# Dealing ratio steps by a fixed table, a later place for the next batch's sigmoids, and an input quantisation without GpSimd

## The chip, the core and the metric

The kernel runs on one core of one Trainium2 chip. The metric is the device time of one execution in microseconds (us). The engines of the core are TensorE (PE in the rows; PEld is its weight load), VectorE (DVE), ScalarE (ACT), GpSimd (POOL) and SyncE (SP, which only issues DMAs). Each works through its own instructions in order, and they wait for one another on semaphores.

## The reference, cut to what matters

Four batches of 512 tokens with 512 channels pass through four sub-layers, each fed by a gate "cond" and each added to x:

```python
x = x + L0_attn(L0_cond(x, f, f, w, u, cond))      # gated linear attention
x = x + L0_ffn(L0_cond2(x, f, f, w, u, cond))      # 16 experts, top 6, plus a shared one
x = x + L1_attn(L1_cond(x, f, f, w, u, cond))      # state space layer, weights quantised to 4 bits
x = x + L1_ffn(L1_cond2(x, f, f, w, u, cond))      # MXFP8 feed-forward
```

Each cond is `sigmoid(x) * ratio`, where the ratio does not depend on x: it is a quotient of exponentials of f, summed by a decaying scan in both directions. The last feed-forward quantises its inputs in blocks of 32:

```python
def _mx_dequant(t):
    blocks = t.reshape(rows, feat // 32, 32)
    scales = maximum(max(abs(blocks), axis=-1) / 448.0, 1e-30)
    q = (blocks / scales[..., None]).astype(float8_e4m3fn).astype(float32)
    return (q * scales[..., None]).reshape(rows, feat)
h = silu(mx(x) @ mx(gate_w).T) * (mx(x) @ mx(up_w).T)
out = mx(h) @ mx(down_w).T
```

## The kernel before

Everything is written out by hand, one instruction stream for each engine. There are three stages.

**Stage 1** is the attention and the routing, batch by batch. The change leaves it alone.

**Stage 2**, from about 1285 to 2435 us, runs 63 expert tiles (`NTL`) of 256 tokens each. In tile j TensorE does these in order: gate and up projections (line 964, 48 matmul records), the input transposes of tile j+1 (L959), the weight transposes of side work (L984), and the down projection of tile j-1 (L975). Two kinds of side work ride along in tiles 0 to 59:

- **Ratio steps.** The second layer's ratios are computed as 16 units of six steps each, 96 in all; `ratio_steps(j)` says which steps belong to tile j. VectorE does `ratio_step(r)`. Steps 0 and 3 start with exponentials from ScalarE (`ratio_exps`, L1245 to L1249, which needs another activation table than the expert's Silu) and go on with four scans; steps 1 and 4 are three elementwise operations; steps 2 and 5 are a reciprocal (L1722), a product, and then the clipped input for the next exponentials (`r_min2` after step 2; `ratio_start` with `r_min` after step 5). So ScalarE's part of step 3 needs VectorE's step 2, and its part of the next unit's step 0 needs VectorE's step 5. Before, 96 steps are spread evenly over 60 tiles, so that a tile has one or two.
- **Preparation of weights.** 74 blocks are quantised and transposed; `prep_tiles(j)` gives one or two of them to a tile. In 14 of the 60 tiles there are two (j = 4, 8, 12, 17, 21, 25, 29, 34, 38, 42, 47, 51, 55, 59). The first 26 blocks have four groups to a row (lighter on VectorE), the rest have blocks of 32. VectorE scales and rounds them in tile j after the ratio steps, and TensorE transposes them in tile j+1. Where there are two, they pass through one PSUM bank: the second transpose waits until ScalarE has copied out the first (L1446).

ScalarE's order in a tile is what the prediction leans on: two Silus, the scaling of this tile's preparation blocks (`scale_groups`, L1402 to L1407, which waits for VectorE's scales), the copies of the next tile's input (L1415), then `ratio_exps`, and only then the copies of the transposed blocks (L1446), and last the expert's output.

**Stage 3**, from about 2435 us on, takes each batch through the state space layer and the feed-forward. The feed-forward has 16 blocks (i = 0 to 15, four groups of weights by four token tiles). For each, TensorE multiplies the gate (L1219) and up (L1225) halves and transposes the previous block's quantised product (L1199); the down projection (L1206) follows in a lump after blocks 5, 9, 13 and at the end. ScalarE does the Silu (L1538) and the copy out of the transposes (L1544). VectorE multiplies (L2301) and quantises (L1652 to L1673). TensorE may begin the gate half of block i+1 only after ScalarE's Silu of block i.

Into this loop the next batch's start is woven: GpSimd gathers the routed expert outputs (`collect`), VectorE sums them (`weigh`, blocks 5, 7, 9, 11) and adds them to x (`add_routed`, L2117, blocks 7, 9, 11, 13), ScalarE takes the sigmoid (`sigmoid2`, L1454, blocks 8, 10, 12, 14), and VectorE multiplies by the ratio (`gate2`).

The feed-forward's own input is quantised in four token tiles before and during the first blocks: TensorE transposes (L1173), VectorE does `quantise_x` up to the addition of the rounding constant (L2294), GpSimd subtracts it again (L1631) and multiplies by the scale (L1636), and TensorE transposes back (L1184).

Of the kernel before, what the change touches and what calls it, by code (L numbers as in the profile page):

```python
# [20 lines left out]
ALU = mybir.AluOpType  # L21
# [3 lines left out]
P = 128  # L25
NB, T, D = 4, 512, 512
NC = D // P
NT = T // P
# [22 lines left out]
QB = 32  # L51
# [76 lines left out]
def build(nc, A, out, scratch_fq, scratch_mx):  # L128
# [11 lines left out]
    with ctx:  # L140
# [226 lines left out]
        f_vx = ev("f_vx", NT)  # L367
        f_qx = ev("f_qx", NT)
# [15 lines left out]
        def r3(ap, n):  # L384
            return ap.rearrange("p (a n) -> p a n", n=n)
# [123 lines left out]

        LAST = NTL - 3  # L510

        def ratio_steps(j):

            a, b = (NB * NC * 6 * min(i, LAST) // LAST for i in (j, j + 1))
            return range(a, b)

        def prep_tiles(j):

# [734 lines left out]
        def _(act):  # L1253
# [198 lines left out]
            def sigmoid2(b, k):  # L1452
                act.wait_ge(x2_ready.sem, x2_ready.at(b, k + 1))
                act.activation(tile_of(hT, k), tile_of(X2[b % 2], k), ACT.Sigmoid).then_inc(sig2.sem, 1)  # L1454
# [4 lines left out]
            for b in range(NB):  # L1459
                act.wait_ge(s_proj.sem, s_proj.at(b, 1))  # L1460
                act.activation(vt, bank(2)[64:64 + SH, :], ACT.Copy).then_inc(s_raw.sem, 1)
                for i in range(2):
                    q = act.activation(bsq[:, i, :], bank(i, SN), ACT.Square)
                q.then_inc(s_sq.sem, 1)
                act.activation(th, bank(2, SN), ACT.Copy)
                act.activation(lamt, bank(2)[96:96 + SH, :], ACT.Sigmoid).then_inc(s_th.sem, 1)
                act.wait_ge(s_v.sem, s_v.at(b, 1))
                act.activation(nab, nab, ACT.Exp)
                act.drain()
                act.activation(nab, nab, ACT.Ln, bias=one[0:SH, :]).then_inc(s_ln.sem, 1)  # L1470
                for i in range(NT * 4):
                    if i == 2:
                        act.wait_ge(s_ms.sem, s_ms.at(b, 1))
                        for q in range(2):
                            mm = act.activation(brs[:, q, :], bank(3 + q, SN), ACT.Sqrt, bias=eps_rms[0:SN, :])
                        mm.then_inc(s_rms.sem, 1)
                        act.wait_ge(s_cs.sem, s_cs.at(b, 1))
                        act.activation(eat, eat, ACT.Exp).then_inc(s_ea.sem, 1)
                    if i == 6:
                        act.wait_ge(s_ang.sem, s_ang.at(b, 1))  # L1480
                        act.activation(trg[:, :, :], nrd[:, :, :], ACT.Sin).then_inc(s_sin.sem, 1)
                    if i == 13:
                        act.wait_ge(s_tmc.sem, s_tmc.at(b, 1))
                        act.activation(eL, csl, ACT.Exp)
                        act.activation(dend, dend, ACT.Exp)
                        act.activation(r3(ecs, SH), tm[:, :, 2, :], ACT.Exp).then_inc(s_exps.sem, 1)
                    k, h = i // 4, i % 2
                    act.wait_ge(s_xz.sem, s_xz.at(b, i + 1))
                    if i % 4 < 2:
                        q = act.activation(xh[k][:, h * 512:(h + 1) * 512], bank(6 + h), ACT.Silu)  # L1490
                    else:
                        q = act.activation(ynT8[:, 4 * h:4 * h + 4, k * P:(k + 1) * P], r3(bank(6 + h), P), ACT.Silu)
                    q.then_inc(s_silu.sem, 1)

                def decay_exp(k, g):
                    act.wait_ge(s_diff.sem, s_diff.at(b, k * 4 + g + 1))
                    act.activation(Md[:, g % 2, :], Md[:, g % 2, :], ACT.Exp).then_inc(s_exp.sem, 1)

                def normalise(k):
                    act.wait_ge(s_yr.sem, s_yr.at(b, k + 1))  # L1500
                    act.activation(Yt[k % 2], Yt[k % 2], ACT.Copy, scale=ss[:, 2:3]).then_inc(s_yn.sem, 1)

                def y_evacuate(k):
                    act.wait_ge(s_tr.sem, s_tr.at(b, k + 1))
                    for i in range(2):
                        q = act.activation(ynT8[:, 4 * i:4 * i + 4, k * P:(k + 1) * P], r3(bank(2 + i), P), ACT.Copy)
                    q.then_inc(s_ynT.sem, 1)

                for k in range(NT):
                    if k:  # L1510
                        normalise(k - 1)
                    decay_exp(k, 0)
                    if k:
                        y_evacuate(k - 1)
                    decay_exp(k, 1)
                    decay_exp(k, 2)
                    decay_exp(k, 3)
                    act.wait_ge(s_y.sem, s_y.at(b, k + 1))
                    act.activation(Dx, Yt[k % 2], ACT.Square, accum_out=ss[:, 0:1])
                    act.drain()  # L1520
                    act.activation(ss[:, 1:2], ss[:, 0:1], ACT.Sqrt, bias=eps_rms, scale=1.0 / DI).then_inc(s_yss.sem, 1)
                normalise(NT - 1)
                y_evacuate(NT - 1)
                for k in range(NT):
                    act.wait_ge(x3_ready.sem, x3_ready.at(b, k + 1))
                    act.activation(tile_of(hT, k), tile_of(X2[b % 2], k), ACT.Sigmoid).then_inc(sig3.sem, 1)

                for i in range(FB * NT + 1):
                    if b + 1 < NB and i >= 8 and i % 2 == 0 and i < 16:
                        sigmoid2(b + 1, (i - 8) // 2)  # L1530
                    if i < NT:
                        act.wait_ge(f_tq.sem, f_tq.at(b, i + 1))
                        act.activation(xqT[:, :, i * P:(i + 1) * P], r3(bank(6), P), ACT.Copy).then_inc(f_xT.sem, 1)
                    if i < FB * NT:
                        act.wait_ge(f_gate.sem, f_gate.at(b, i + 1))
                        if i >= 2:
                            act.wait_ge(f_mul.sem, f_mul.at(b, i - 1))
                        act.activation(fs[i % 2], bank(4), ACT.Silu).then_inc(f_silu.sem, 1)  # L1538
                    if i:
                        ib, t = (i - 1) // NT, (i - 1) % NT  # L1540
                        act.wait_ge(f_tr.sem, f_tr.at(b, i))
                        if t == 0 and ib >= 2:
                            act.wait_ge(f_down.sem, f_down.at(b, ib - 1))
                        act.activation(hqT[ib % 2][:, :, t * P:(t + 1) * P], r3(bank(6), P), ACT.Copy)\  # L1544
                           .then_inc(f_hT.sem, 1)


        @block.gpsimd
        def _(pool):
# [41 lines left out]
            def collect(b):  # L1591

                for n in range(NTK):
                    k = b * NTK + n
                    if k >= NYG:
                        pool.wait_ge(y_acc.sem, k - NYG + 1)
                    pool.indirect_dma_start(yg[k % NYG], None, d_y,
                                            bass.IndirectOffsetOnAxis(ap=physu[:, k:k + 1], axis=0))\
                        .then_inc(y_rows[k % NYG].sem, 16)
# [6 lines left out]
            for b in range(NB):  # L1606
# [18 lines left out]
                        per_head(state, state, eL[0:SN, hs]).then_inc(s_sdec.sem, 1)  # L1625


                for t in range(NT):
                    v, m = fxv[t % 2], fxm[t % 2]
                    pool.wait_ge(f_vx.sem, f_vx.at(b, t + 1))  # L1630
                    pool.tensor_tensor(v, v, m, ALU.subtract)  # L1631
                    pool.drain()
                    if t >= 2:
                        pool.wait_ge(f_tq.sem, f_tq.at(b, t - 1))
                    sc = fxamx[t % 2][:, 16:32].unsqueeze(2).to_broadcast([P, 16, QB])
                    pool.tensor_tensor(r3(fqx[t % 2], QB), r3(v, QB), sc, ALU.mult).then_inc(f_qx.sem, 1)  # L1636
                if b + 1 < NB:
                    collect(b + 1)


        @block.vector
        def _(dve):
            tt, ts, stt = dve.tensor_tensor, dve.tensor_scalar, dve.scalar_tensor_tensor

            def bcast(ap, n):

                return ap.unsqueeze(2).to_broadcast([ap.shape[0], ap.shape[1], n])
# [485 lines left out]
            for b in range(NB):  # L2133
# [152 lines left out]

                def quantise_x(t):
                    dve.wait_ge(f_tx.sem, f_tx.at(b, t + 1))
                    if t >= 2:
                        dve.wait_ge(f_qx.sem, f_qx.at(b, t - 1))  # L2290
                    v, m = fxv[t % 2], fxm[t % 2]
                    quantise_head(bank(7), v, m, fxamx[t % 2])
                    dve.drain()
                    tt(v, v, m, ALU.add).then_inc(f_vx.sem, 1)  # L2294

                quantise_x(0)
                quantise_x(1)
# [91 lines left out]
```

## Time and profile before

| what | value |
|---|---|
| device time, median of 3 runs | 4275.18 us (4270.21 to 4276.04) |
| the profiled execution: its own time, its span | 4278.56 us, 4276.8 us |
| PE busy | 3637.4 us, 85% of the span |
| DVE busy | 2588.9 us, 61% |
| ACT busy | 1194.1 us, 28% |
| POOL busy | 558.0 us, 13% |
| mean granted TensorE clock | 0.896 of full speed |

Durations and starts in the rows come from the profiled execution, which took 3.4 us longer than the median of the timed runs. "Idle before <- releaser" is the time that an engine stood still ahead of an instruction and what ended it.

### The profile page before, as it was taken

Reading aid. Unit: us, or ns where it says so; the run is one execution under the profiler, and the core shown is the slowest. Engines: PE = TensorE matmul, PEld = TensorE weight load, DVE = VectorE, ACT = ScalarE, POOL = GpSimd, SP = SyncE. Lnnn points to the kernel's source line nnn. Section 1 sums busy time; section 2 is a strip of 40 time slices with the busy share of each in tenths; the row PEclk is TensorE's granted clock in tenths of the full one; section 3 lists DMA queues with packets and bytes.
Section 4 is the critical chain, followed back from the end, with each engine's and each line's share of the span. In section 5 each row is a group of like instructions: output and inputs, shape, how many; then the busy total and the mean of one; then the engine's idle time right before and its main releaser. Section 6 shows DMA issues by size and latency. Waiting matters only on the chain.

```text
span 4276.8 us, 38855 instructions
## 1 busy us (share of the span) xinstructions
PE 3637.4 (85%) x13526; PEld 2272.7 (53%) x13526; DVE 2588.9 (61%) x3690; ACT 1194.1 (28%) x1974; POOL 558.0 (13%) x451
## 2 busy tenths in 40 slices
PE   2887887787879999998999779789979898889988
PEld 1653644545537777776776536543654356434743
DVE  5877877877845556776677344564346344644454
ACT  1332332323304444333333222212221222113210
POOL 1003002021021111110111112110212011201100
PEclk9989888889989999999999977899779887998799
DMA  3212202102117667666666510122013201221011
GB/s 142 60 31 61 68 18 74 55 18 72 38 33 258 211 230 236 219 229 197 230 220 226 187 74 30 69 103 79 30 55 117 79 30 54 74 105 48 1 59 40
DMA packets 277843, 444.62 MB, mean 104 GB/s; under 512 B 52560, under 2 KB 189776, under 8 KB 265104
## 3 DMA queue, kind: packets, MB, share of 16 engines
q1 hardware_dynamic: 256768, 383.74, 27.1%
q0 software_dynamic: 20880, 58.40, 4.3%
q8 instruction: 108, 1.77, 0.2%
q14 instruction: 87, 0.71, 0.1%
HBM read 368.49 MB, written 97.70 MB: 109 GB/s over the span
## 4 chain that ended last, share of the span: by engine, by line
PE 59%; DVE 20%; issue 9%; DVEq 5%; ACT 4%; DMA 2%; POOL 1%; POOLq 0%; SPq 0%; ACTq 0%
PE bank L964 14%; PE bank L975 7%; PE bank L1206 5%; PE bank L1219 5%; PE bank L1225 4%; PE bank L782 3%; PE bank L1073 3%; DVE sb_gla L1793 2%; DVE sb_ratio L1768 2%; DVEq L1774 2%; PE bank L1114 2%; PE bank L1092 1%; PE bank L759 1%; DVE sb_work L1805 1%; PE bank L762 1%
## 5 line engine op out<-in xcount | busy, mean ns | idle before, releaser
L964 PE MATMUL bank<-sb_xT,sb_work 128*128 128x256 f32 x3024 | 665.4, 380 | 1.6 <-issue 0.8
L964 PEld LDWEIGHTS bank<-sb_xT,sb_work 128*128 128x128 f32 x3024 | 576.0, 191 | 106.8 <-issue 31.3
L782 PE MATMUL bank<-sb_gla,sb_work 128*128 128x256 f32 x896 | 261.7, 445 | 111.7 <-DVE sb_work L1795 99.1
L975 PE MATMUL bank<-sb_work,sb_hT 128*128 128x512 f32 x756 | 351.0, 616 | 0.0
L1219 PE MATMUL bank<-sb_parts,sb_small 128*128 128x512 f32 x512 | 257.1, 649 | 43.8 <-ACT sb_work L1538 39.0
L782 PEld LDWEIGHTS bank<-sb_gla,sb_work 128*128 128x128 f32 x896 | 189.9, 219 | 174.8 <-DVE sb_work L1795 120.2
L762 PE MATMUL bank<-sb_hT,sb_work 128*128 128x512 f32 x384 | 180.5, 618 | 101.4 <-DVE sb_hT L1742 101.4
L1587 POOL DMA_INDIRECT sb_parts<-scratch_h,sb_small x126 | 136.0, 1079 | 983.3 <-DMA sb_small<-scratch_ids 963.8
L1073 PE MATMUL bank<-sb_parts,sb_hT 128*128 128x512 f32 x512 | 238.6, 627 | 0.0
L1206 PE MATMUL bank<-sb_work,sb_parts 128*128 128x512 f32 x512 | 233.5, 616 | 2.7 <-ACT sb_work L1544 2.7
L975 PEld LDWEIGHTS bank<-sb_work,sb_hT 128*128 128x128 f32 x756 | 145.9, 200 | 161.4 <-issue 161.4
L1225 PE MATMUL bank<-sb_parts,sb_small 128*128 128x512 f32 x512 | 230.2, 592 | 0.0
L1793 DVE TENSOR_TENSOR sb_gla<-sb_gla,sb_work 128x1024 f32<-128x1024 f32 x112 | 147.7, 1319 | 132.8 <-PE bank L782 126.9
L922 PE MATMUL bank<-sb_work,sb_parts 128*128 128x512 f32 x384 | 177.7, 619 | 38.7 <-ACT sb_small L1392 28.7
L2301 DVE TENSOR_TENSOR sb_work<-sb_work,bank 128x512 f32<-128x512 f32 x64 | 44.0, 688 | 244.8 <-PE bank L1225 229.1
L1219 PEld LDWEIGHTS bank<-sb_parts,sb_small 128*128 128x128 f32 x512 | 102.8, 210 | 161.9 <-issue 121.5
L2087 DVE TENSOR_TENSOR sb_hT<-sb_parts,bank 128x256 f32<-128x256 f32 x63 | 26.6, 422 | 261.6 <-PE bank L964 258.4
L2221 DVE TENSOR_TENSOR sb_work<-bank,sb_work 128x512 f32<-128x512 f32 x64 | 44.1, 690 | 225.4 <-PE bank L1083 137.4
L1575 POOL DMA_INDIRECT scratch_ids<-sb_small x96 | 107.2, 1117 | 553.5 <-DVE sb_small L1951 525.5
L1073 PEld LDWEIGHTS bank<-sb_parts,sb_hT 128*128 128x128 f32 x512 | 101.8, 201 | 134.1 <-issue 130.5
L762 PEld LDWEIGHTS bank<-sb_hT,sb_work 128*128 128x128 f32 x384 | 74.7, 199 | 183.3 <-DVE sb_hT L1742 104.0
L1206 PEld LDWEIGHTS bank<-sb_work,sb_parts 128*128 128x128 f32 x512 | 100.1, 198 | 125.7 <-issue 121.4
(363 smaller groups left out, 6113.3 us busy)
## 6 DMA issues: line engine op xcount, KB each, us to landing
sb_work<-scratch_gu SPq DMA_DIRECT2D x63, 1408.0 KB, 7.5
sb_parts<-scratch_mx SPq DMA_DIRECT2D x16, 3072.0 KB, 10.4
sb_work<-moe_w SPq DMA_DIRECT2D x63, 512.0 KB, 5.1
scratch_y<-sb_work SPq DMA_DIRECT2D x63, 512.0 KB, 6.8
sb_parts<-scratch_fq SPq DMA_DIRECT2D x24, 1024.0 KB, 7.9
sb_work<-w_qkvg SPq DMA_DIRECT2D x64, 256.0 KB, 2.6
scratch_gu<-moe_w SPq DMA_DIRECT2D x32, 512.0 KB, 5.8
sb_parts<-fT SPq DMA_DIRECT2D x48, 256.0 KB, 3.7
```

What stands on the lines that cost most here:

```text
L762: mm = pe.matmul(dst, gw[:, m, k, :], ch(hT, k), start=(k == 0), stop=(k == NC - 1))
L782: mm = pe.matmul(dst.rearrange("p (h n l) -> p h n l", h=HPC, l=size), kS[u % 2][:, k * P:(k + 1) * P], late[:, :, k, :, 1, :], start=True ...
L922: mm = pe.matmul(bank(4 + which), shw[j][:, a:a + P], ch(h1, k), start=(k == 0), stop=(k == NC - 1))
L964: mm = pe.matmul(dst, egu[j % 3][:, which * NC + k, m * P:(m + 1) * P], xt[j % 2][:, k, :], start=(k == 0), stop=(k == NC - 1))
L975: mm = pe.matmul(bank(YB[s]), einter[j % 2][:, m * SLOTS + s * P:m * SLOTS + (s + 1) * P], edn[j % 3][:, m * D:(m + 1) * D], start=(m == 0 ...
L1073: mm = pe.matmul(bank(6 + i % 2), ch(hT, kk)[:, k * P:(k + 1) * P], wzx[:, m, kk, :], start=(kk == 0), stop=(kk == NC - 1))
L1206: mm = pe.matmul(bank(oc), fw[ib % 2][:, 2, i, oc * P:(oc + 1) * P], hqT[ib % 2][:, i, :], start=(ib == 0 and i == 0), stop=(ib == FB - 1 ...
L1219: mm = pe.matmul(bank(4), xqT[:, k, t * P:(t + 1) * P], fw[ib % 2][:, 0, k, :], start=(k == 0), stop=(k == NC - 1))
L1225: mm = pe.matmul(bank(5), xqT[:, k, t * P:(t + 1) * P], fw[ib % 2][:, 1, k, :], start=(k == 0), stop=(k == NC - 1))
L1575: pool.indirect_dma_start(d_ids, bass.IndirectOffsetOnAxis(ap=slot_u[b % 2][:, i:i + 1], axis=0), tokid[:, tk:tk + 1], None).then_inc(ids_ ...
L1587: pool.indirect_dma_start(hg[j % 2][:, s, :], None, d_h, bass.IndirectOffsetOnAxis(ap=idx[j % 4][:, s:s + 1], axis=0))\
L1793: tt(late, late, now2[:, :, 0].unsqueeze(1).unsqueeze(3).to_broadcast([P, HPC, n, size]), ALU.mult)
```

## The change

It has three parts, and it computes the same values.

1. `ratio_steps` reads a table. A unit of six steps gets four tiles, with steps [0, 1], [2], [3, 4] and [5]; every fourth unit (n = 0, 4, 8, 12) gets three tiles, with [0, 1], [2] and [3, 4, 5]. The units fill tiles 0 to 59 as before; the three-step tiles are 2, 17, 32 and 47.
2. ScalarE's `sigmoid2(b + 1, ...)` moves from the head of round i of the feed-forward loop to its foot, behind the Silu of block i and the copy of block i-1.
3. VectorE does the two operations on the quantised input that GpSimd did. The wait for the reuse of the buffer moves with them. GpSimd goes to `collect(b + 1)` after the first token tile's rounding instead of after the fourth's scaling.

```diff
+        ratio_at = []
+        for n in range(NB * NC):
+            cuts = (0, 2, 3, 5, 6) if n % 4 else (0, 2, 3, 6)
+            ratio_at += [range(6 * n + a, 6 * n + e) for a, e in zip(cuts, cuts[1:])]
+
         def ratio_steps(j):
-            a, b = (NB * NC * 6 * min(i, LAST) // LAST for i in (j, j + 1))
-            return range(a, b)
+            return ratio_at[j] if j < LAST else ()
...
                 for i in range(FB * NT + 1):
-                    if b + 1 < NB and i >= 8 and i % 2 == 0 and i < 16:
-                        sigmoid2(b + 1, (i - 8) // 2)
                     if i < NT:
...
                         act.activation(hqT[ib % 2][:, :, t * P:(t + 1) * P], r3(bank(6), P), ACT.Copy)\
                            .then_inc(f_hT.sem, 1)
+                    if b + 1 < NB and i >= 8 and i % 2 == 0 and i < 16:
+                        sigmoid2(b + 1, (i - 8) // 2)
...
-                for t in range(NT):
-                    v, m = fxv[t % 2], fxm[t % 2]
-                    pool.wait_ge(f_vx.sem, f_vx.at(b, t + 1))
-                    pool.tensor_tensor(v, v, m, ALU.subtract)
-                    pool.drain()
-                    if t >= 2:
-                        pool.wait_ge(f_tq.sem, f_tq.at(b, t - 1))
-                    sc = fxamx[t % 2][:, 16:32].unsqueeze(2).to_broadcast([P, 16, QB])
-                    pool.tensor_tensor(r3(fqx[t % 2], QB), r3(v, QB), sc, ALU.mult).then_inc(f_qx.sem, 1)
                 if b + 1 < NB:
+                    pool.wait_ge(f_vx.sem, f_vx.at(b, 1))
                     collect(b + 1)
...
                 def quantise_x(t):
                     dve.wait_ge(f_tx.sem, f_tx.at(b, t + 1))
-                    if t >= 2:
-                        dve.wait_ge(f_qx.sem, f_qx.at(b, t - 1))
                     v, m = fxv[t % 2], fxm[t % 2]
                     quantise_head(bank(7), v, m, fxamx[t % 2])
                     dve.drain()
                     tt(v, v, m, ALU.add).then_inc(f_vx.sem, 1)
+                    dve.drain()
+                    tt(v, v, m, ALU.subtract)
+                    dve.drain()
+                    if t >= 2:
+                        dve.wait_ge(f_tq.sem, f_tq.at(b, t - 1))
+                    tt(r3(fqx[t % 2], QB), r3(v, QB), bcast(fxamx[t % 2][:, 16:32], QB), ALU.mult)\
+                        .then_inc(f_qx.sem, 1)
```

## Rows read from the trace of the kernel before

**Rows 1.** The page's chain that ended last, shares of the span by engine
```profile
PE 59%; DVE 20%; issue 9%; DVEq 5%; ACT 4%; DMA 2%; POOL 1%; POOLq 0%; SPq 0%; ACTq 0%
```

**Rows 2.** Timeline of PE, expert stage: start, length, line [idle before <- releaser]
```profile
1302.15 10.60 PE L964 MATMUL bank<-sb_xT,sb_work 128*128 128x256 f32 x48 [0.79 <-issue]
...
1592.11 10.52 PE L964 MATMUL bank<-sb_xT,sb_work 128*128 128x256 f32 x48
...
1608.93 10.52 PE L964 MATMUL bank<-sb_xT,sb_work 128*128 128x256 f32 x48
...
1627.27 10.52 PE L964 MATMUL bank<-sb_xT,sb_work 128*128 128x256 f32 x48
...
2414.48 10.52 PE L964 MATMUL bank<-sb_xT,sb_work 128*128 128x256 f32 x48
```

**Rows 3.** Timeline of PE and ACT around tiles 30 and 35
```profile
1823.68 10.52 PE L964 MATMUL bank<-sb_xT,sb_work 128*128 128x256 f32 x48
...
1835.78 1.28 ACT L1248 ACT_TABLE_LOAD   x1
...
1837.61 0.61 ACT L1249 ACTIVATE sb_ratio<-sb_work 128x512 f32<-128x512 f32 x1
...
1838.85 1.09 PE L984 MATMUL bank<-sb_const,sb_parts 128*128 128x128 f32 x4 [3.34 <-ACT sb_parts L1446]
...
1845.90 10.52 PE L964 MATMUL bank<-sb_xT,sb_work 128*128 128x256 f32 x48
...
1913.19 10.52 PE L964 MATMUL bank<-sb_xT,sb_work 128*128 128x256 f32 x48
...
1927.86 1.11 PE L984 MATMUL bank<-sb_const,sb_parts 128*128 128x128 f32 x4 [2.83 <-DVE sb_parts L2077]
...
1936.50 10.52 PE L964 MATMUL bank<-sb_xT,sb_work 128*128 128x256 f32 x48
```

**Rows 4.** Timeline of tile 51 on DVE (steps 3, 4, preparation) and PE's transposes
```profile
2224.47 0.42 DVE L2087 TENSOR_TENSOR sb_hT<-sb_parts,bank 128x256 f32<-128x256 f32 x1 [4.84 <-PE bank L964]
...
2236.49 0.43 DVE L2070 TENSOR_SCALAR sb_parts<-sb_parts 128x512 uint32<-128x512 uint32 x1
...
2238.53 0.69 DVE L2077 TENSOR_TENSOR sb_parts<-sb_parts 128x512 f32<-128x512 f32 x1
...
2240.97 0.69 DVE L2054 TENSOR_TENSOR sb_parts<-sb_parts 128x512 f32<-128x512 f32 x1
...
2241.91 0.60 PE L984 MATMUL bank<-sb_const,sb_parts 128*128 128x128 f32 x4
```

**Rows 5.** Timeline of DVE, tile 29: step 5 from its reciprocal to the next work
```profile
1821.96 3.35 DVE L1722 RECIPROCAL sb_ratio<-sb_ratio 128x512 f32<-128x512 f32 x1
...
1827.16 0.43 DVE L2070 TENSOR_SCALAR sb_parts<-sb_parts 128x512 uint32<-128x512 uint32 x1
```

**Rows 6.** Timeline of the feed-forward's input: POOL, and PE waiting for it
```profile
2716.77 1.26 POOL L1631 TENSOR_TENSOR sb_work<-sb_work 128x512 f32<-128x512 f32 x1 [47.37 <-DVE sb_work L2294]
...
2721.28 1.05 POOL L1636 TENSOR_TENSOR sb_work<-sb_work 128x512 f32<-128x512 f32 x1 [3.25 <-issue]
2722.38 1.11 PE L1184 MATMUL bank<-sb_const,sb_work 128*128 128x128 f32 x4 [10.27 <-POOL sb_work L1636]
...
2744.94 0.66 PE L1184 MATMUL bank<-sb_const,sb_work 128*128 128x128 f32 x4 [4.03 <-POOL sb_work L1636]
...
3171.93 1.11 PE L1184 MATMUL bank<-sb_const,sb_work 128*128 128x128 f32 x4 [9.13 <-POOL sb_work L1636]
```

**Rows 7.** Timeline of batch 0's feed-forward: blocks 8 and 12, and the last
```profile
2819.84 0.63 ACT L1454 ACTIVATE sb_hT<-sb_xT 128x512 f32<-128x512 f32 x1 [9.64 <-DVE sb_xT L2117]
...
2822.43 6.57 PE L1219 MATMUL bank<-sb_parts,sb_small 128*128 128x512 f32 x8 [6.42 <-ACT sb_work L1538]
...
2876.11 5.34 PE L1219 MATMUL bank<-sb_parts,sb_small 128*128 128x512 f32 x8 [6.71 <-ACT sb_work L1538]
...
2919.93 1.11 PE L1199 MATMUL bank<-sb_const,sb_work 128*128 128x128 f32 x4 [5.84 <-DVE sb_work L1673]
```

More of the change, by code:

```diff
@@ L510, in build @@
         LAST = NTL - 3
+        ratio_at = []
+        for n in range(NB * NC):
+            cuts = (0, 2, 3, 5, 6) if n % 4 else (0, 2, 3, 6)
+            ratio_at += [range(6 * n + a, 6 * n + e) for a, e in zip(cuts, cuts[1:])]
+        assert len(ratio_at) == LAST
         def ratio_steps(j):
-            a, b = (NB * NC * 6 * min(i, LAST) // LAST for i in (j, j + 1))
-            return range(a, b)
+            return ratio_at[j] if j < LAST else ()
         def prep_tiles(j):
```

## The prediction, made before any run of the changed kernel

> **What bounds the kernel now.** I read the page first, then the two stages that the diff touches on TensorE's timeline. The chain that ended last lies 59% on PE and 20% on DVE [rows 1]: TensorE is the engine to watch, and what counts is where it stands still. In the expert stage it has a steady beat. Tile 17 starts at 1592.11 and tile 18 at 1608.93, 16.82 us later, with PE busy throughout; tile 18 has a second weight transpose and ends at 1627.27, so a tile with a pair costs 18.34, that is 1.52 more [rows 2]. From tile 1 (1302.15) to tile 62 (2414.48) there are 61 tiles in 1112.33 us. 61 x 16.82 is 1026.0, and 14 pairs add 21.3. **So 65 us are lost to stalls**, all of which sit in front of the transposes L984. In the feed-forward of stage 3 PE stands at four kinds of places: for GpSimd's two operations at the start, 10.27 us in batch 0 and 9.13 later, and 4.03 at the third token tile [rows 6]; for the Silu that stands behind the next batch's sigmoid, 6.42 and 6.71; and for the last block's quantisation, 5.84 [rows 7].
>
> **Part 1, the table.** What it removes: the tiles in which ScalarE's exponentials need a VectorE step of the same tile (steps 2 and 3, or 5 and 0). Counting the old formula, 12 of 60 tiles have that, and six of them fall on a tile in which PE transposes a pair (9, 13, 26, 39, 43, 56). There PE waits long, since ScalarE stands in `ratio_exps` with the copy L1446 queued behind it. These six make most of the 65 us.
>
> What it adds is seen in tile 30, the one old pair tile with exponentials that are ready: nothing crosses there, and PE still waits 3.34 us [rows 3]. ScalarE first loads the table (starts 1835.78, 1.28 us), does the exponentials, the last from 1837.61, and copies only then. The tile took 1845.90 - 1823.68 = 22.22, or 3.88 over a plain pair; part of this is a clock that fell after the wait, since the matmuls behind it are slower. In the old deal the pairs at 5, 18, 22, 48 and 60 had no exponentials and were free or nearly so. In the new table I lay the pairs beside the steps: PE's pair tiles 5, 9, 13, 35, 39, 43 all have [3, 4], and 18, 22, 26, 30, 48, 52, 56 all have [0, 1]. Only 60 is free. So 13 of 14 pairs pay:
>
> - Five with [0, 1] and nothing else (22, 26, 30, 52, 56): 3.88 each, 19.4.
> - Six with [3, 4]: one exponential fewer (0.6 us), so at least 3.3. The upper end is tile 35, which paid 1936.50 - 1913.19 - 18.34 = 4.97 after a wait of 2.83, the length that I expect here [rows 3]. I take 3.8, nearer to tile 30, whose wait has the same cause: 22.8.
> - Tile 48, behind the three-step tile 47. VectorE's time from the tile's first product to the end of step 4 is 2236.49 - 2224.47 = 12.02 [rows 4]; step 5 adds 1827.16 - 1821.96 = 5.20 [rows 5]; rounding and new scales for the first block add 2241.66 - 2236.49 = 5.17 [rows 4]. That is 22.4. ScalarE's scaling in tile 48 waits for those scales, and behind it stand the input copies (about 1.7 us with the scaling, an estimate) and table, exponentials and copy (3.07, from 1835.78 to PE's start at 1838.85 [rows 3]): 27.2. PE wants the second transpose at 17.44 (2241.91 - 2224.47 [rows 4]) plus 1.5. It is 8.3 late, plus 2 for the clock: 10.3.
> - Tile 18, behind 17, has the same chain with lighter blocks: 9 (estimate).
> - Tile 33, behind 32, has one block: ready at 17.22 + 2.73 (2239.22 - 2236.49) = 19.95, wanted at 17.44; 2.5 late and 1.7 for the clock: 4.2.
> - Tiles 1 and 3, where VectorE gets an extra step ahead of its first blocks: together about 3.5 (estimate).
>
> Sum 69 against the 65 that go: **the table gives nothing, +4 us**. The bounds: with the pairs at 3.3 and the clock terms at nothing 57, with those eleven at tile 35's price 82; so from -8 to +17.
>
> The Trainium skill, ScalarE: Activation LUTs, "What ACT_TABLE_LOAD costs", charges a switch of tables with a drain of about 1.38 us beside the 1.28 of the load. By this rule each of the 13 paying pairs would be later by 1.38 and the sum higher by 18 us. The trace doesn't show it: between 1835.78 and 1837.61 lie the load and one exponential of 0.6 and nothing more [rows 3], and I stay with the row.
>
> **Part 2, the sigmoid.** At block 8 ScalarE waits 9.64 us for VectorE's L2117 before the sigmoid at 2819.84, then reloads Silu's table; PE gets its gate half at 2822.43, after 6.42 idle [rows 7]. Moved, Silu 8 runs as soon as its gate half is there, and PE goes on at about 2816.0. What is late next is VectorE: it is free only at 2819.8. It multiplies block 8 by 2820.6, which holds PE's up half of block 9 for some 1.3 us, and its quantised block is there 5.5 us later (the last block shows 5.84 from PE's end to the transpose [rows 7]), at 2826.1, which holds the transpose for 2.1. Before, this transpose came at 2832.3 (2822.43 + 6.57 for the slowed gate half + 3.4 for the up half), so 6 are won. Block 12 goes the same way and wins 4.5 (its gate half took 5.34, less slowed). The waits at blocks 10 and 14 lie beneath the down projection and are worth nothing. The sigmoid itself is wanted by VectorE one quantisation later, and is in time. That is 10.5 a batch; the two new waits in a row may lower the clock under the down projection, 1.5 each time. I take 9, with 5 to 11 as bounds, in three batches: **-27 us (-33 to -15)**.
>
> **Part 3, the input.** VectorE's addition ended at 2716.69, GpSimd's first operation started at 2716.77 and took 1.26, then 3.25 of "issue", then 1.05, and PE started at 2722.38 [rows 6]. VectorE's elementwise operations on the same shape take 0.69 (as L2077 [rows 4]) with 0.08 between: done at 2718.23, so 4.0 us are won in batch 0. In batch 1 PE's wait is 9.13, 1.1 shorter, so 2.9 there and in 2 and 3. At the third token tile (wait 4.03) the same exchange gives about 1; VectorE now carries 1.5 us more for each of tiles 2 and 3 ahead of its product, which PE wants later by more than that, so nothing is taken back but some 0.5 in batch 0. Sum: 4.7 + 3 x 4.1 = **-17 us (-20 to -12)**. GpSimd's gathers start some 40 us sooner. They ended before VectorE asked for them already, so this gives nothing; VectorE asks first at block 5.
>
> **Sum.** +4 - 27 - 17 = -40. The profiled execution's own time is 4278.56 (span 4276.8, 1.8 around it), which gives 4238.6; the median is 3.4 lower, so **4235 us**.
>
> **Rivals.**
> - *The table does what it seems made for.* Pair tiles with ready exponentials are free, and only 18, 33 and 48 cost (about 22). Then part 1 gives -43 and the time is 4188. For it: the long waits all have the crossing. Against it: tile 30. Chance 0.07.
> - *VectorE becomes the bound of the feed-forward.* If its sums and quantisations set the pace from block 7 on, PE's waits return as waits for L1673 and part 2 gives only 2 us a batch: 4235 + 21 = 4256. For it: VectorE is free only 4 us after PE could go on. Against: after blocks 9 and 13 the down projection gives VectorE room. Chance 0.12.
> - *The clock, and slower.* Fifteen short stalls replace ten. If each kept PE at the lower of its two levels (1.2 and not 2.4 GHz) through the next tile's projections, whose 10.5 us would then cost 5 more on a cautious count, the sum would be 4235 + 75 = 4310. It decides from 3.3 us a stall on (49 / 15). Against it: the groups that follow the stalls at 1845.90 and 1936.50 took 10.52, as ever [rows 3]. Chance 0.03.
> - *Parts 2 and 3 are eaten* (a gather or a wait of VectorE in the way), which leaves the time within 0.2%, about what a measurement of this kernel can tell from no change: 0.03.
>
> The forecast itself has 0.75. Range: part 1's bounds carry most; with VectorE's rival inside, 4212 to 4256. The forecast's own range is 4218 to 4250. Faster 0.93, within 0.2% 0.04, slower 0.03.
>
> **What would show it.** The old pair tiles 9, 13, 26, 39, 43, 56 fall to 22 us; 5, 22, 35, 52 rise to 22; 18 and 48 take 27 to 29, with PE released by L1446; tile 33 waits for L2077. From tile 1 to 62 about 1116 us. In the feed-forward no gate half waits 6 us; L1199 waits for L1673 at blocks 8 and 12 for some 2. PE's first L1184 waits about 6.2 us. If 13 pairs are free, or if stage 2 moves by more than 20 us either way, my reading of ScalarE's queue is wrong.

## The result, and the profile after

| what | before | after |
|---|---|---|
| device time, median | 4273.01 us (4270.21 to 4276.04, 4 runs) | 4210.8 us (4204.48 to 4216.69, 4 runs) |
| the recorded execution: its own time, its span | 4278.56, 4276.8 us | 4204.48, 4202.6 us |
| mean granted clock | 0.896 | 0.909 |

The changed kernel is faster: ratio 0.9853, 95% interval 0.9841 to 0.9865. That is 62 us where 40 were forecast, and 1.2 us below the lower end of the range. The forecast started from 4275.18 for before, 2.2 us above the median here, so the range was missed by less than that median moved; the 22 us beyond the forecast are far more than that. The recorded execution of after is 6 us quicker than its median and the one of before 5.5 us slower than its own, so the traces lie 74 us apart and not 62. For that reason the stages are compared first, and each against more than one execution.

Cut by TensorE's timeline, the two recorded executions look like this (us; "state space" runs from the stage's first projection to the first transpose of the feed-forward's input, "feed-forward" from there to the next stage):

| stretch | before | after | forecast of the difference |
|---|---|---|---|
| tile 1 to tile 62 | 1112.3 | 1116.8 | +4 |
| feed-forward, batches 0 to 3 | 229.7, 229.5, 229.4, 213.6 | 215.5, 213.1, 213.3, 210.2 | -44 |
| state space, batches 1 to 3 | 221.0, 221.1, 221.1 | 213.9, 216.5, 216.4 | 0 |
| state space, batch 0 | 223.7 | 213.0 | 0 |

The first row came out as forecast (+4.5; how much of that is luck is said further down), the second is -50, and the other two, -16.4 and -10.7, are in code that the change leaves alone. The rest of the span makes up the last 1.5.

**The expert stage.** After, timeline of TensorE and ScalarE around tile 30, which pairs two transposes with steps [0, 1]; it answers to [rows 3]:

```profile
1828.98 10.52 PE L969 MATMUL bank<-sb_xT,sb_work 128*128 128x256 f32 x48
...
1841.08 1.28 ACT L1253 ACT_TABLE_LOAD   x1
...
1842.37 0.63 ACT L1253 ACTIVATE sb_ratio<-sb_small 128x512 f32<-128x512 f32 x1
...
1842.91 0.61 ACT L1254 ACTIVATE sb_ratio<-sb_work 128x512 f32<-128x512 f32 x1
...
1844.15 1.09 PE L989 MATMUL bank<-sb_const,sb_parts 128*128 128x128 f32 x4 [3.34 <-ACT sb_parts L1451]
...
1852.56 10.52 PE L969 MATMUL bank<-sb_xT,sb_work 128*128 128x256 f32 x48
```

It is the same picture as before the change, to the hundredth: 3.34 us of waiting. The tile takes 1852.56 - 1828.98 = 23.6. The same wait of 3.34 stands in tiles 22, 26, 52 and 56, and one of 2.82 in the six with [3, 4]. Tile 48, behind the three-step tile, from the same view:

```profile
2156.56 10.52 PE L969 MATMUL bank<-sb_xT,sb_work 128*128 128x256 f32 x48
...
2172.83 0.63 ACT L1412 ACTIVATE sb_parts<-sb_parts 128x512 f32<-128x512 f32 x1 [8.78 <-DVE sb_parts L2051]
...
2174.45 1.28 ACT L1253 ACT_TABLE_LOAD   x1
...
2177.53 1.09 PE L989 MATMUL bank<-sb_const,sb_parts 128*128 128x128 f32 x4 [6.26 <-ACT sb_parts L1451]
...
2184.80 10.52 PE L969 MATMUL bank<-sb_xT,sb_work 128*128 128x256 f32 x48
```

ScalarE is held at the scaling until 2172.83 by VectorE's scales, then the input copies, the table and the exponentials pass, and TensorE's second transpose comes 6.26 us late: 28.2 us for the tile. In TensorE's waits (us in total, times, longest) the table shows as hardly anything. First before, then after:

```profile
PE bank L984 <- ACT sb_parts L1446: 52.8, 12, 12.1
```

```profile
PE bank L989 <- ACT sb_parts L1451: 47.4, 14, 6.6
...
PE bank L1189 <- DVE sb_work L2295: 37.9, 9, 6.2
PE bank L1204 <- DVE sb_work L1670: 34.8, 10, 6.2
...
PE bank L989 <- DVE sb_parts L2074: 5.2, 2, 2.8
...
PE bank L989 <- DVE sb_parts L2064: 3.2, 3, 1.4
```

The longest wait halved, but there are more of them. What VectorE held (`<- DVE`) was 4.9 us before and is 5.2 and 3.2 now. No gate half (L1224) waits for the Silu behind a sigmoid any more, and the transposes L1204 now wait ten times instead of four.

**The feed-forward.** After, timeline of batch 0: the first input transpose, the blocks 8 and 9, and the last block; it answers to [rows 6, 7]:

```profile
2710.52 1.12 PE L1189 MATMUL bank<-sb_const,sb_work 128*128 128x128 f32 x4 [6.19 <-DVE sb_work L2295]
...
2808.37 0.68 DVE L2303 TENSOR_TENSOR sb_work<-sb_work,bank 128x512 f32<-128x512 f32 x1
2808.48 0.63 ACT L1459 ACTIVATE sb_hT<-sb_xT 128x512 f32<-128x512 f32 x1 [1.90 <-DVE sb_xT L2114]
2809.10 3.70 PE L1230 MATMUL bank<-sb_parts,sb_small 128*128 128x512 f32 x8 [1.02 <-DVE sb_work L2303]
...
2814.75 0.66 PE L1204 MATMUL bank<-sb_const,sb_work 128*128 128x128 f32 x4 [1.95 <-DVE sb_work L1670]
...
2815.68 15.60 PE L1211 MATMUL bank<-sb_work,sb_parts 128*128 128x512 f32 x32
...
2898.73 1.11 PE L1204 MATMUL bank<-sb_const,sb_work 128*128 128x128 f32 x4 [5.84 <-DVE sb_work L1670]
2900.53 15.97 PE L1211 MATMUL bank<-sb_work,sb_parts 128*128 128x512 f32 x32 [0.69 <-ACT sb_work L1547]
```

The wait for the sigmoid, 6.42 us, has become two short ones for VectorE, 1.02 and 1.95. The sigmoid still waits for VectorE's sum, but by now nothing stands behind it that TensorE wants. The down projection after them shows a lowered clock here (15.60 against 13.90 for the same group in before). The input transpose waits 6.19 in place of 10.27.

**The state space layer.** Busy time of each engine in batch 2's state space stage. The columns are the stretch, its length, the busy time of PE, PEld, DVE, ACT and POOL with their instructions, the granted clock, the share of the DMA engines and GB/s. Before, and then after:

```profile
3391.61:3612.69 221.08, 203.86 (x788) 126.13 (x789) 93.89 (x127) 66.12 (x92) 27.78 (x14) 0.82 0.10 37
```

```profile
3346.15:3562.67 216.52, 198.00 (x789) 122.47 (x789) 93.97 (x127) 66.14 (x92) 27.80 (x14) 0.83 0.10 37
```

The same work is issued, and VectorE, ScalarE and GpSimd are busy as long as before. TensorE alone is busy for 5.9 us less, at a higher clock. The two timelines have the same groups with 15 waits between them. Thirteen of these are equal to 0.03 us; one, for VectorE's part at L2187, is even longer (1.96 for 0.27), since TensorE comes to it sooner, and one is 3.60 for 3.96. For the rest the two differ in which groups are slow. The first projections of the stage, before and after:

```profile
3391.61 12.29 PE L1035 MATMUL bank<-sb_hT,sb_work 128*64 128x512 f32 x24 [2.67 <-DVE sb_xT L2318]
```

```profile
3346.15 10.68 PE L1040 MATMUL bank<-sb_hT,sb_work 128*64 128x512 f32 x24 [2.66 <-DVE sb_xT L2320]
```

### The profile page after: what moved, and what is told of

It reads as the page before. It is cut to its first block, busy times and chain, and to the rows that moved or that the text cites. A ratio compares the mean times of both kernels' runs of the same rounds, so it can differ in the third digit from the quotient of the medians.

```text
span 4202.6 us, 38866 instructions
## 1 busy us (share of the span) xinstructions
PE 3598.4 (86%) x13526; PEld 2246.8 (53%) x13526; DVE 2610.6 (62%) x3722; ACT 1197.0 (28%) x1974; POOL 524.1 (12%) x419
## 4 chain that ended last, share of the span: by engine, by line
PE 62%; DVE 22%; DVEq 5%; ACT 4%; issue 3%; DMA 2%; POOL 1%; SPq 0%; ACTq 0%; POOLq 0%
PE bank L969 14%; PE bank L980 8%; PE bank L1211 5%; PE bank L1224 4%; PE bank L1230 4%; PE bank L787 3%; PE bank L1119 3%; PE bank L1078 3%; DVE sb_gla L1790 2%; PE bank L1097 2%; DVE sb_ratio L1765 2%; DVEq L1771 2%; PE bank L1155 1%; PE bank L767 1%; PE bank L764 1%
## 5 line engine op out<-in xcount | busy, mean ns | idle before, releaser
L1224 PE MATMUL bank<-sb_parts,sb_small 128*128 128x512 f32 x512 | 244.2, 622 | 4.5 <-ACT sb_small L1536 4.5
L1230 PE MATMUL bank<-sb_parts,sb_small 128*128 128x512 f32 x512 | 230.8, 593 | 5.9 <-DVE sb_work L2303 5.9
L1078 PE MATMUL bank<-sb_parts,sb_hT 128*128 128x512 f32 x512 | 228.7, 605 | 0.0
```

The lines of the kernel that those rows point to most:

```text
L1078: mm = pe.matmul(bank(6 + i % 2), ch(hT, kk)[:, k * P:(k + 1) * P], wzx[:, m, kk, :], start=(kk == 0), stop=(kk == NC - 1))
L1224: mm = pe.matmul(bank(4), xqT[:, k, t * P:(t + 1) * P], fw[ib % 2][:, 0, k, :], start=(k == 0), stop=(k == NC - 1))
L1230: mm = pe.matmul(bank(5), xqT[:, k, t * P:(t + 1) * P], fw[ib % 2][:, 1, k, :], start=(k == 0), stop=(k == NC - 1))
```

## The experiments

All ratios are to the kernel before, on the same chip. Stage lengths are from the recorded execution of each.

### The parts alone

The unchanged kernel against itself tells what the measurement can resolve.

> The kernel before, unchanged. In the changed kernel's trace the state space stages, whose code nobody touched, took 213.0, 213.9, 216.5 and 216.4 us against 223.7, 221.0, 221.1 and 221.1 before, 27 us in all. Theory A (chance of the clock in one recorded execution): the same code recorded again shows state space stages that differ from 221 to 224 by several us, and its timed runs spread by 5 us or more. Theory B (something in the change speeds them up each time): the same code gives 221 to 224 again, within 1 us. Ratio 1.000 by both.

Measured: 0.9994 (0.9985 to 1.0002). Its stages are those of before, except one: batch 0's state space stage took 217.2 us and not 223.7. So 6.5 us of a trace's difference there can come with no change of code at all. Batches 1 to 3 repeat to 0.1 us.

Part 1 alone: only `ratio_steps` reads the table.

> The kernel before with the ratio table alone. My sum: the expert stage (start of tile 1 to start of tile 62) goes from 1112.3 to 1116.8, as in the changed kernel, so the ratio is 1.001. Rival (the table gains what the crossings cost, and the recorded execution hides it): 0.990. Theory B for the state space stages says that they show whether this part speeds them up: 221 each if not, 213 to 216 if so.

Measured: 1.0002 (0.9992 to 1.0012); the expert stage took 1110.7 us. The pairs' waits are the same to 0.02 us as in after. What differs is how much clock they cost. The kernels with the table and ScalarE's old order took 1110.5 to 1116.8 for the same code, those with the even deal 1111.2 to 1112.9. The table gives nothing, and costs nothing that these runs can tell.

Part 2 alone:

```diff
                 for i in range(FB * NT + 1):
-                    if b + 1 < NB and i >= 8 and i % 2 == 0 and i < 16:
-                        sigmoid2(b + 1, (i - 8) // 2)
...
                            .then_inc(f_hT.sem, 1)
+                    if b + 1 < NB and i >= 8 and i % 2 == 0 and i < 16:
+                        sigmoid2(b + 1, (i - 8) // 2)
```

> The kernel before with the sigmoids moved alone. My sum: 9 us in each of three feed-forwards, 27 us, ratio 0.9937; with the measured feed-forwards of the changed kernel (-14.2, -16.4, -16.1 and -3.3 in the last, which has no sigmoids) the share of this part is about -12 a batch, 36 us, 0.9916. Expert stage 1112. State space stages 221 if this part does not act on them, 213 to 216 if it does.

Measured: 0.9894 (0.988 to 0.9907), 45 us, more than either of the two expected sums. The feed-forwards of batches 0 to 2 gave 12.5, 12.2 and 11.3 us (36), the state space stages of batches 1 to 3 another 1.5, 2.5 and 4.7 (8.7). Timeline of TensorE in this kernel, batch 0, blocks 9 and 13 and the last:

```profile
2827.37 3.70 PE L1225 MATMUL bank<-sb_parts,sb_small 128*128 128x512 f32 x8 [1.02 <-DVE sb_work L2301]
2833.03 0.66 PE L1199 MATMUL bank<-sb_const,sb_work 128*128 128x128 f32 x4 [1.96 <-DVE sb_work L1673]
2833.95 13.90 PE L1206 MATMUL bank<-sb_work,sb_parts 128*128 128x512 f32 x32
...
2880.37 0.66 PE L1199 MATMUL bank<-sb_const,sb_work 128*128 128x128 f32 x4 [1.73 <-DVE sb_work L1673]
2881.30 13.90 PE L1206 MATMUL bank<-sb_work,sb_parts 128*128 128x512 f32 x32
...
2917.45 15.48 PE L1206 MATMUL bank<-sb_work,sb_parts 128*128 128x512 f32 x32 [0.69 <-ACT sb_work L1542]
```

From the previous block's transpose to the start of the down projection before had 17.73 us at block 9 and 16.79 at block 13; here it is 2833.95 - 2822.31 = 11.64 and 2881.30 - 2869.61 = 11.69. So 6.1 and 5.1 are won. Both down projections take 13.90, as before, and the last one 15.48 in place of 16.71. Together 12.4.

Part 3 alone: `quantise_x` and GpSimd's loop as in the change, the rest as before.

> The kernel before with the input quantised by VectorE alone and the earlier gathers. My sum: 17 us, ratio 0.9960; the last feed-forward of the changed kernel, which has this part alone, gave only 3.3, so four of them 13 us, 0.9969. State space stages 221 if this part does not act on them. If it does, by gathers that are out of the way or by GpSimd reaching its own work sooner, 213 to 216 and a ratio near 0.991.

Measured: 0.9945 (0.9932 to 0.9957), 23.5 us, between the expected sums and the rival. The feed-forwards gave 5.8, 2.0, 5.5 and 2.4 (15.7). The state space stages of batches 1 and 3 gave 2.4 and 2.5, that of batch 2 nothing.

Parts 2 and 3 without the table:

> The changed kernel with the old dealing of the ratio steps. The table alone gave 1.0002, so my theory (its stalls only change places) says that this one equals the changed kernel within 0.15%: ratio 0.984 to 0.986, expert stage 1112 against 1117. Rival (the table pays only beside the other two parts): 0.988 or more. Interaction of the other two: alone they gave 0.9894 and 0.9945, which multiply to 0.9840; if the clock's gains are counted twice it is above 0.986.

Measured: 0.9847 (0.9833 to 0.986), as fast as the whole change. The feed-forwards took 850.6 us in all, the state space stages of batches 1 to 3 216.4, 216.5 and 216.4. So the whole gain is that of parts 2 and 3, and they nearly add: 45 and 23.5 alone, 65 together.

### What the pairs wait for

The forecast put down the waits in the pair tiles to ScalarE's queue: the copy that frees the bank stands behind `ratio_exps`. To test it, all but the last of a tile's copies go ahead of the exponentials, once with the table and once with the even deal (both with parts 2 and 3).

```diff
+                ready = list(prep_tiles(j - 1))
+                for i in ready[:-1]:
+                    act.wait_ge(prep_t.sem, i + 1)
+                    if i >= 2:
+                        act.wait_ge(prep_st[i % 2].sem, 16 * (i // 2))
+                    act.activation(pt_[i % 2], bank(7), ACT.Copy).then_inc(prep_c.sem, 1)
                 for r in ratio_steps(j):
                     if r % 3 == 0:
                         ratio_exps(act, N1 + r // 6, r % 6 == 3)
-                for i in prep_tiles(j - 1):
+                for i in ready[-1:]:
```

> The changed kernel, but where ScalarE has two transposed blocks to copy out in a tile, the first is copied ahead of the ratio's exponentials and not behind them. If the waits of 2.82 and 3.34 us in 13 tiles are this queue on ScalarE, they fall to 0.88 (tiles 18 and 48, where the scaling waits for VectorE, keep 3 to 5 us), and the expert stage goes from 1117 to about 1064: 61 x 16.82 + 14 x 1.5 + 17 = 1064; ratio about 0.973. Rival (the waits are VectorE's lateness, which shows under ScalarE's name): the stage stays above 1100 and the waits turn to L2074 or L2064.

> The same reordering with the old dealing. By my theory the six long waits of tiles with crossing steps (5.8 to 12.1 us) were the same queue, so they go as well, and only the tiles where VectorE is late (35, 52 and 30) keep something, 10 us in all: stage about 1057, ratio 0.972, as good as with the table. Rival (the crossing itself costs, since ScalarE stands in it and all behind it is late): stage 1085 or more, the table is worth 0.5% or more once the queue is mended.

Measured: 0.972 (0.9707 to 0.9733) and 0.9722 (0.9709 to 0.9735). The expert stage fell to 1067.3 us with the table and to 1054.3 without. The even deal, timeline of ScalarE and TensorE in tile 30, the one of [rows 3]:

```profile
1819.36 0.60 ACT L1444 ACTIVATE sb_parts<-bank 128x512 f32<-128x512 f32 x1
1819.98 1.28 ACT L1248 ACT_TABLE_LOAD   x1
1820.11 0.63 PE L984 MATMUL bank<-sb_const,sb_parts 128*128 128x128 f32 x4 [0.88 <-ACT sb_parts L1444]
```

The copy runs at once, the table is loaded behind it, and TensorE waits 0.88 us in place of 3.34. The total, from the waits of TensorE:

```profile
PE bank L984 <- ACT sb_parts L1444: 10.5, 11, 1.3
```

So 42 of the 52.8 us came from the copy's place, and neither from the crossing nor from the loads, which are all still there. Some 3 of the 42 come back as a wait for VectorE's block in tile 39 (L2075: 7.7 us in three tiles, where before had 4.9 in two). With the copy in front the even deal needs no help: its stage is 13 us shorter than the table's, whose tiles 18 and 48 still wait (4.18 and 4.64 us). The two medians agree all the same, 4160.4 and 4161.1. In the two recorded executions batch 0's state space stage takes back the difference (211.6 with the table, 223.2 without); whether it does so in the others is not shown.

### What the clock gives

The gain in untouched code is one of TensorE's clock. First theory: a stage runs faster when TensorE was kept busier ahead of it. To the kernel after were added matmuls on constants, which compute nothing that is used, in three waits of each feed-forward.

```diff
                 x_transpose(0)
+                spin(bank(0), 6)
                 xq_transpose(0)
...
+                        if i == 1:
+                            pe.wait_ge(f_silu.sem, f_silu.at(b, 2))
+                            spin(bank(4), 3)
...
+                pe.wait_ge(f_silu.sem, f_silu.at(b, FB * NT))
+                spin(bank(4), 6)
                 f_transposes(FB * NT - 1)
```

Here `spin(dst, n)` is n matmuls of 512 columns from the constants into a bank that is free then. Each of them shows as two records in the trace, so that six appear as x12.

> The changed kernel with matmuls on constants (written to banks that nobody reads) in three of TensorE's waits of each feed-forward: six in the wait for the first quantised input (6.2 us), three in that of the third token tile (3.0), six in that for the last quantised block (5.8); 0.86 us each at full clock. Work is added, none is taken out. If the state space stages' 213 to 224 us are made by where the clock stands low, then the clock now stays up, the slowed groups behind the waits (5.84, 4.83, 15.97 and 10.68 us) go to 3.6, 3.6, 13.9 and 10.4, feed-forwards get 3 to 6 us shorter each and state space stages come to 213 or less: ratio to before 0.975 to 0.981. Rival (not the clock, but the order of instructions or DMAs): feed-forwards the same or longer and state space stages unchanged, 0.985 or more.

Measured: 0.9821 (0.9808 to 0.9835). The feed-forwards took 841.7 us in place of 852.1, the state space stages of batches 1 to 3 212.2, 210.5 and 219.5. Two of these came down as the theory has it, the third is longer than in after (216.4), and the ratio is just above the expected 0.975 to 0.981.

Then the same in the kernel before, and in after only the last of the three places.

> The kernel before, with the same matmuls on constants put into TensorE's waits in the feed-forward (6 ahead of the first transposes back, 3 ahead of the second tile's, 6 ahead of the last block's transposes), and no part of the change. Theory (the clock of a stage depends on how TensorE was kept before it): the second and third state space stage, 221.0 and 221.1 us in every execution without parts 2 and 3, come down to 211 to 217 us without any edit to them, and the feed-forwards gain 2 to 3 us each; together 15 to 25 us, a ratio of 0.994 to 0.9965. Rival (the state space stages are shorter because GpSimd gathers sooner and VectorE has less standing in its queue, that is through parts 2 and 3 themselves): they stay at 221.0 and 221.1, and the ratio is 0.998 or more.

Measured: 0.9971 (0.996 to 0.9982). The feed-forwards gave 12 us, as they should, but the state space stages of batches 2 and 3 stood at 220.9 and 221.0, and batch 1's took 223.8. On these stages the rival is right: filled waits do not by themselves shorten the stage behind.

> The kernel after, with matmuls on constants only in the wait ahead of the last block's transposes of each feed-forward (6 of them, behind the last Silu). Theory (the clock): the 5.8 and 4.8 us waits go beneath work and the groups behind run at the higher clock, so each feed-forward is 2 to 3 us shorter, and the state space stages behind move too, by up to 5 us each; ratio 0.983 to 0.985. Rival: all of what the added matmuls gave came from the waits at the feed-forward's start, and this one gives nothing: 0.985 to 0.986.

Measured: 0.9794 (0.9782 to 0.9807), more than either theory allowed, and better than the three places together. Timeline of TensorE in this kernel, the last block of batch 0 and then of batch 1:

```profile
2898.56 5.32 PE L1245 MATMUL bank<-sb_const 128*128 128x512 f32 x12
2904.56 0.66 PE L1204 MATMUL bank<-sb_const,sb_work 128*128 128x128 f32 x4 [0.69 <-DVE sb_work L1673]
2905.90 14.00 PE L1211 MATMUL bank<-sb_work,sb_parts 128*128 128x512 f32 x32 [0.69 <-ACT sb_work L1550]
...
3321.89 5.32 PE L1245 MATMUL bank<-sb_const 128*128 128x512 f32 x12
3328.25 0.66 PE L1204 MATMUL bank<-sb_const,sb_work 128*128 128x128 f32 x4 [1.04 <-DVE sb_work L1673]
3329.59 15.70 PE L1211 MATMUL bank<-sb_work,sb_parts 128*128 128x512 f32 x32 [0.69 <-ACT sb_work L1550]
```

In batches 0, 2 and 3 the wait for VectorE fell from 5.84 to 0.69, the transpose behind it took 0.66 instead of 1.11, and the down projection 14.0 instead of 15.9 to 16.7: the added work lies beneath the wait, and the clock stays up. Batch 1 is the exception. Its wait fell from 6.19 to 1.04, but the down projection kept its slow 15.70 (15.65 in after). From the transposes ahead of the added work to the end of the stage the four batches won 2.4, 0.4, 2.3 and 3.2 us, 8.3 in all. The feed-forwards as a whole gave 8.5: batch 0 won another 2.2 ahead of the place, and batch 1 lost 2.5 there, again in code that is the same. The state space stages of batches 1 to 3 gave 14 more: 210.2, 210.5 and 212.1. Of the waits in batch 2's, none is shorter than in after by more than 0.01 us. Batch 2's in the same view as above:

```profile
3347.96:3558.45 210.49, 191.28 (x789) 117.87 (x789) 93.87 (x127) 66.13 (x92) 27.79 (x14) 0.87 0.10 38
```

Three kernels, one stage, the same instructions and 93.9 to 94.0 us of VectorE in each: 221.08 at a granted clock of 0.82, 216.52 at 0.83, 210.49 at 0.87.

The other explanation on offer was the gather, which part 3 starts earlier. Held back until the fourth token tile is scaled:

```diff
-                    pool.wait_ge(f_vx.sem, f_vx.at(b, 1))
+                    pool.wait_ge(f_qx.sem, f_qx.at(b, NT))
                     collect(b + 1)
```

> The kernel after, with GpSimd's gather for the next batch held back until VectorE has scaled the fourth token tile, about where it stood before. Theory (the earlier start of the gather is worth nothing): 0.984 to 0.986, VectorE still finds the gathered rows there at block 5. Rival (part of what part 3 gave, and of the state space stages' gain, is the earlier gather): 0.987 to 0.990.

Measured: 0.985 (0.9837 to 0.9863). The first gather of batch 0 starts at 2746.38 and not at 2709.19. The stages of batches 1 to 3 are 216.4, 216.5 and 216.4, the feed-forwards 850.6, as in the kernel without the table. The gather's start is worth nothing, in either place.

### The fastest version

Parts 2 and 3, the copies first, the even deal, and the matmuls in the three waits:

> Parts 2 and 3 with the even deal of before, the first copies of a tile ahead of ScalarE's exponentials, and the matmuls on constants in the feed-forward's waits. If the two add: 0.972 - 0.003 = 0.969, about 4148 us, faster than the kernel after by 1.6%. If both draw on the same reserve of clock: 0.972.

Measured: 4135.77 us, 0.9683 (0.9671 to 0.9696), 1.7% faster than the changed kernel (0.9683 / 0.9853). Its expert stage is that of the copies first (1054.3), its feed-forwards are those of the filled waits (841.6): the two add. With the last place alone, which did better in after, it was not run.

## Why the prediction came out as it did

**Part 1 was right in its mechanism and its sum.** It was "13 of 14 pairs pay". They do. Term by term, as excess over 16.82 or 18.34: five pairs with [0, 1] 24.1 (19.4 forecast), six with [3, 4] 19.3 (22.8), tile 48 9.9 (10.3), tile 18 9.1 (9), tile 33 4.7 (4.2), tiles 1 and 3 2.7 (3.5). The sum is 70 against 69. That it meets to 1 us is in part luck. With the table alone every one of these waits is the same to 0.02 us, and the sum is 64, since fewer of them lowered the clock. The waits themselves came as read (3.34 and, for tile 35's kind, 2.82 where 2.83 was expected); the two group errors are the clock behind them. One sign was misread: tile 35 was said to rise to 22 us, but it had taken 23.3 before, by the forecast's own rows, and fell to 21.6. The Trainium skill, ScalarE: Activation LUTs, "What ACT_TABLE_LOAD costs", would have had each of them later by 1.38; the rows of tile 30 go against it once more, load at 1841.08, exponential at 1842.37.

**Part 2 was right in its mechanism and too small.** All rows stand where they were put: the up half's wait 1.02 (1.3 forecast), the transpose's 1.95 (2.1), no gate half that waits. "That is 10.5 a batch" measured 11.2. The first step that failed is the one behind it: "the two new waits in a row may lower the clock under the down projection, 1.5 each time. I take 9". The part alone shows 13.90 under both, and 1.2 won under the last one. In after one of the six such groups of the three batches was indeed slowed (15.60, in batch 0), the others not. So the term was 12.0 a batch in the kernel with this part alone and not 9, -36 and not -27. The lower bound of -33 failed with it, since it took the arithmetic of the waits as the best case, and gave the clock only the power to take away.

**Part 3 was right in its mechanism and its sum.** -17 forecast, -15.7 in the feed-forwards; the wait 6.19 where 6.2 was said. The split was not: 4.7 and three times 4.1 were forecast, and 5.8, 2.0, 5.5 and 2.4 came. GpSimd's gathers gave nothing either way.

**What the sum left out is the state space layer.** This is the second step that failed, and the larger one: these stages were put at nothing, and the forecast gives no reason for it; the change touches none of their instructions. In the executions with both parts and nothing else in the feed-forward it is 14 to 16 us shorter in batches 1 to 3, and this makes most of the distance between 40 and 62: it is 14, part 2's missing 3 a batch are 9, and part 3 takes back 1. The steadiness of these stages shows that it is not chance. They took 221.0 or 221.1 in all three recorded executions without part 2 or 3 and without added work, 216.4 or 216.5 in the four kernels with parts 2 and 3 in which the table is left out, the gather held back or the copies first (in after itself 213.9, 216.5 and 216.4), and 212.2, 210.5 and 219.5 in both kernels with three filled places. What picks the slow groups was not settled. It is not the gather; it is not simply how busy TensorE was kept, since filled waits made these stages no shorter in before, and in after 4 to 6 us shorter with the last place filled but one of three longer with all three places filled. That the lengths depend on what came ahead, by 10.6 us in batch 2, is shown; by what rule, stays open. The recorded gain of batch 0's stage (10.7) is not the change's: the unchanged kernel's own executions differ there by 6.5, and kernels with the same code up to that point took from 213.0 to 222.4.

**The rivals.** VectorE did not become the bound: it holds TensorE for 3 us at a block and nothing after. The table does not do what it seems made for. The clock rival named the right cause with the wrong sign: 15 stalls did not cost 3.3 us each, and the clock gave time back where the forecast only let it take some. The range of 4212 to 4256 was built from the bounds of the edited places alone, and therefore reached only 23 us below the forecast; with a term for the clock in the stages behind, as large below as above, it would have held the result.

## What to carry to other kernels

When an engine waits for another's copy, read that engine's timeline and see what is queued ahead of the copy. Here moving a copy ahead of the exponentials was worth 52 us (4213 to 4161), and another deal of the exponentials nothing. A removed stall can be worth more than its length, through the clock and partly in stages that nobody edited (31 us of waits, by the forecast's arithmetic, gave 45); give this a term of both signs in the range, and compare stages over several executions before calling such a difference the change's. A wait that cannot be removed can still be filled with work that keeps the clock up, but measure each place by itself.

## What the runs showed of the hardware

- TensorE's clock moved a whole stage of unchanged instructions between 210.2 and 223.8 us (granted 0.87 to 0.80), and the stage with the higher clock had the longer waits in sum (21.1 us in batch 2 with the last wait filled, 19.1 in before). Within one kernel batches 1 to 3 repeat to 0.1 us in some kernels and differ by up to 9 us in others (210.5 and 219.5). The Trainium skill, TensorE: Matmul & The Clock Gate, "Part 1: The HAM clock gate", says that the slow matmuls at a kernel's start vary from run to run and prices the ramp at under 1% of a span. Batch 0's stage agrees with the first in kind, though far from the start (217.2 and 223.7 in two executions of one code). The second is about the start alone, which no run here measures. Far from the start the clock makes 5% of one stage (10.6 us in batch 2), and the three places with added matmuls are worth 0.3% of the whole.
- Matmuls whose result nobody reads, 6 to 15 in a feed-forward, made the kernel faster by up to 0.6% (0.9794 against 0.9853).
- One and the same wait costs unlike amounts of clock. In the kernel after, five waits of 3.34 us, 2.46 over the 0.88 of a free pair, lengthened their tiles by 4.0 to 5.5 us; six of 2.82, 1.94 over it, by 3.3 to 3.6 in five tiles and by 1.9 in the sixth, where the clock cost nothing.
